# Self-attention and group norm on one core: all later row tiles in high/low parts, low parts on GpSimd, f and g in one step, y over x

## The chip, the cores and the metric

One core of a Trainium2 chip. Its engines are TensorE (matmuls, PE in the profile), VectorE (DVE), ScalarE (ACT), GpSimd (POOL) and SyncE (SP, which only issues transfers here). The metric is the device time of one execution in microseconds; lower is better.

## The reference

Eight images of 128 channels and 32 x 32 = 1024 positions, float32. First self-attention with a residual, then a group norm whose groups are found from the data.

```python
xf = x.reshape(B, Cc, N)                                  # B = 8, Cc = 128, N = 1024
x_f = jnp.einsum('oc,bcn->bon', Wf, xf) + bf[None, :, None]      # 16 rows
x_g = jnp.einsum('oc,bcn->bon', Wg, xf) + bg[None, :, None]      # 16 rows
x_h = jnp.einsum('oc,bcn->bon', Wh, xf) + bh[None, :, None]      # 128 rows
s = jnp.einsum('bci,bcj->bij', x_f, x_g)
beta = jax.nn.softmax(s, axis=-1)
x = x + gamma[0] * jnp.einsum('bci,bij->bcj', x_h, beta).reshape(B, Cc, H, W)
...
x_n = x_flat / jnp.maximum(nrm, 1e-12)
cos = jnp.einsum('bcn,bdn->cd', x_n, x_n) / B             # channels against channels
_, idx = jax.lax.top_k(-jnp.abs(cos).T, k)                # k = 4: the partners of a channel
mean, var over each channel and its 3 partners, per image
x_hat = (x - mean) * rsqrt(var + EPS);  out = gamma * x_hat + beta
```

## The kernel before, in words

The order on every engine is written out by hand, with semaphores between the engines. The images go one after the other; the stage of an image b has T = 8 steps t, one for each row tile of 128 rows of the 1024 x 1024 score matrix.

A row tile passes through these steps. TensorE scores it (`score`, two matmuls of 128x512 into one of two PSUM buffers `s_ps`). VectorE takes the negated row maximum (`row_max`). ScalarE takes exp with the row sum (`exp`, into `probs`). VectorE inverts the sum (`invert_sum`). The values of the tile are scaled by it, and TensorE multiplies them with the probabilities and adds to `o_ps` (`attend`). TensorE scores AHEAD = 3 tiles before the one it attends.

There are two forms of attend. A whole tile uses float32 operands: ScalarE scales the values (`scale_values`, into `vnorm`), and TensorE goes over each half in a slow float32 matmul. A split tile, here tiles 3 and 7 of each image (`SPLIT`), uses high and low parts in fp32r: ScalarE copies `probs` to `probs_high` (`high_part`), VectorE computes `probs_low = probs - probs_high`, `v_high = values * rinv` and `v_low = values * rinv - v_high` (`split_parts`), and TensorE does three fast products per half.

Beside the tiles a stage does the next image's projections into the PSUM tensor `w_ps`: f and g in one matmul per half (`project_fg`), which ScalarE copies to `fg32` (with the bias) and again, negated and masked, to `fg_neg`; g's rows are then added on VectorE (`parts`), f's rows on GpSimd (`parts_f`). The values of the next image follow (`project_values`, `add_value_bias`). For the previous image it does the residual (`residual`, from `x_all` to `y_all`), the squares and their norm (ScalarE and GpSimd, `nsq` and `rnorm`), and the product of y with itself: transposes, `yT` in a high part (ScalarE) and a low part (VectorE, `low_part`), `gram`, `scale_gram`, `turn_gram`, `add_gram`. After the last image the partners are found, and the shifted and scaled y is stored.

Of the kernel before, what the change touches and what calls it, by code (L numbers as in the profile page):

```python
# [37 lines left out]
P = 128  # L38
BANK = 512
AHEAD = 3  # L40
SCALED = 2
SPLIT = (3, 7)
# [9 lines left out]

def build(nc, x, wide, out):
# [4 lines left out]
    assert C == P and H == 2 and T == 8 and B % 2 == 0 and B >= 4  # L58
    assert all(SCALED <= t < T for t in SPLIT)

    with ExitStack() as ctx:
# [9 lines left out]
        x_all = sb("x_all", [P, B, N])  # L71
        y_all = sb("y_all", [P, B, N])
        wd = sb("wd", [P, WIDE])
        warm = sb("warm", [P, BANK], BF16)
        fg32 = sb("fg32", [P, N])
        fg_neg = sb("fg_neg", [P, N], F32R)
        f_parts = [sb(f"f_parts{i}", [P, N], F32R) for i in range(2)]
        g_parts = [sb(f"g_parts{i}", [P, N], F32R) for i in range(2)]
        values = [sb(f"values{i}", [P, T, P]) for i in range(2)]
        probs = [sb(f"probs{i}", [P, N]) for i in range(T)]  # L80
        vnorm = [sb(f"vnorm{i}", [P, P]) for i in range(T)]

        probs_high = [sb(f"probs_high{i}", [P, N], F32R) for i in range(len(SPLIT))]
        probs_low = [sb(f"probs_low{i}", [P, N], F32R) for i in range(len(SPLIT))]
        v_high = [sb(f"v_high{i}", [P, P], F32R) for i in range(len(SPLIT))]
        v_low = [sb(f"v_low{i}", [P, P], F32R) for i in range(len(SPLIT))]
# [43 lines left out]
        zeros_set = sem("zeros_set")  # L130

        fg_proj = sem("fg_proj")
        fg_copied = sem("fg_copied")
        neg_ready = sem("neg_ready")
        g_ready = sem("g_ready")
        f_head = sem("f_head")
        f_ready = sem("f_ready")
# [12 lines left out]
        probs_used = sem("probs_used")  # L150
# [31 lines left out]
        TH = T // H  # L182
        L = B - 1
# [8 lines left out]
        WHOLE = [t for t in range(T) if t not in SPLIT]  # L192

        def ahead(b, t, par):

            return (b, t, par) if t < T else (b + 1, t - T, 1 - par)

        def split_count(b, t):
            return len(SPLIT) * b + SPLIT.index(t) + 1

        def whole_count(b, t):
            return len(WHOLE) * b + WHOLE.index(t) + 1

        def run_stages(stage):

            for b in range(B):
                stage(b, b % 2, first=b == 0, previous=b > 0, turn=b > 1, project=b < L)

# [3 lines left out]
        def _(sp):  # L212
            for h in range(H):
                sp.dma_start(x_all[:, 0, halves[h]], x[0][:, halves[h]]).then_inc(head_in[h], 16)
            for b in range(1, B):
                if b == 2:

                    sp.wait_ge(const_in, 16)
                sp.dma_start(x_all[:, b, :], x[b]).then_inc(x_in[b], 16)
            sp.wait_ge(v_out, 1)  # L220
            sp.dma_start(out[0][:, halves[0]], y_all[:, 0, halves[0]]).then_inc(stored, 16)
            sp.wait_ge(a_head, 1)
            sp.dma_start(out[0][:, halves[1]], y_all[:, 0, halves[1]]).then_inc(stored, 16)
            for n, b in enumerate(VEC_IMAGES):
                sp.wait_ge(v_out, n + 2)
                sp.dma_start(out[b], y_all[:, b, :]).then_inc(stored, 16)
# [3 lines left out]
        def _(pool):  # L230
            nc.gpsimd.memset(mhalf[:, :], -0.5).then_inc(halves_set, 1)
            pool.wait_ge(halves_set, 1)

            def parts_f(b):
                for h in range(H):
                    pool.wait_ge(neg_ready, H * b + h + 1)
                    if b >= 2:

                        pool.wait_ge(scores, T * (b - 1))
                    nc.gpsimd.tensor_tensor(f_parts[b % 2][0:KP, halves[h]], fg32[0:KP, halves[h]],  # L240
                                            fg_neg[0:KP, halves[h]].bitcast(F32), ALU.add).then_inc(f_ready, 1)


            pool.wait_ge(neg_ready, H)
            pool.wait_ge(zeros_set, 4)
            nc.gpsimd.tensor_tensor(f_parts[0][0:KP, halves[1]], fg32[0:KP, halves[1]],
                                    fg_neg[0:KP, halves[1]].bitcast(F32), ALU.add).then_inc(f_ready, 1)
            for b in range(B):
                if b == 0:
                    parts_f(1)  # L250
# [509 lines left out]
```

## Time and profile before

| | |
|---|---|
| median of 3 runs | 213.6 us (213.32 to 213.78) |
| profiled execution, its own time | 213.6 us |
| its span | 211.8 us |
| one middle image | 22.2 us |
| TensorE busy | 88% of the span |
| VectorE busy | 82% |
| ScalarE busy | 68% |
| GpSimd busy | 16% |

The span is what the profiler recorded between the first and the last instruction of one execution; 1.8 us of the execution's own time lie outside it. Busy shares are averages over the head (loads and the first image), the middle and the tail, which have different limits.

### The profile page before, as it was taken

What the parts mean: (1) busy time and instruction counts of PE and PEld (TensorE: products, weight loads), DVE (VectorE), ACT (ScalarE), POOL (GpSimd) and SP (SyncE); (2) the same over time, 40 slices, a digit from 0 to 9 for tenths busy, and PEclk for the clock granted to TensorE, in tenths of its full rate; (3) what the DMA queues carried; (4) which work ended last, traced back from release to release, by engine and by line L of the source; (5) the groups of instructions that cost most, each with busy time, mean ns of one, the idle gap of its engine ahead of it and who ended that gap; (6) DMA issues with size and microseconds to landing.
All of it is one profiled execution on the core that took longest, in us unless ns stands there. A gap on an engine that the chain in (4) does not pass through costs nothing.

```text
span 211.8 us, 2308 instructions
## 1 busy us (share of the span) xinstructions
PE 187.0 (88%) x727; PEld 115.9 (55%) x727; DVE 174.3 (82%) x317; ACT 144.4 (68%) x256; POOL 34.4 (16%) x39
## 2 busy tenths in 40 slices
PE   7599979999999999999999999999999999983100
PEld 2454546465765676566756675667566756371000
DVE  6678989979898889989898989888988898766650
ACT  2548976799379955995599658985799378740320
POOL 0200210034003400160007000520034001001400
PEclk9969999999999999999999999999999999996555
DMA  5880000000000000000000000000000000000198
GB/s 209 315 330 0 0 3 0 3 0 0 0 3 0 0 0 0 0 3 2 0 0 2 0 0 3 0 0 0 0 3 2 0 0 0 0 3 2 57 400 335
DMA packets 2892, 8.87 MB, mean 42 GB/s; under 512 B 320, under 2 KB 448, under 8 KB 2880
## 3 DMA queue, kind: packets, MB, share of 16 engines
q1 hardware_dynamic: 2304, 7.34, 9.0%
q10 hardware_dynamic: 576, 1.38, 1.7%
q8 instruction: 6, 0.10, 0.2%
q14 instruction: 6, 0.05, 0.1%
HBM read 4.52 MB, written 4.19 MB: 41 GB/s over the span
## 4 chain that ended last, share of the span: by engine, by line
PE 73%; DVE 11%; ACT 6%; issue 5%; POOL 1%; DVEq 0%; ACTq 0%; POOLq 0%
PE o_ps L602 40%; PE s_ps L583 12%; PE w_ps L572 7%; PE w_ps L577 6%; PE w_ps L617 3%; PE w_ps L611 2%; DVE nmax L376 2%; ACT probs L292 2%; PE o_ps L569 2%; DVE y_all L562 1%; DVE probs_low L390 1%; DVE g_parts L399 1%; DVE y_all L414 1%; ACT probs_high L298 1%; ACT fg_neg L285 1%
## 5 line engine op out<-in xcount | busy, mean ns | idle before, releaser
L292 ACT ACTIVATE probs<-s_ps,nmax 128x1024 f32<-128x1024 f32 x64 | 71.0, 1109 | 40.4 <-DVE nmax L376 40.2
L602 PE MATMUL o_ps<-probs,vnorm 128*128 128x512 f32 x192 | 89.9, 592 | 0.5 <-DVE y_all L414 0.5
L376 DVE TENSOR_REDUCE nmax<-s_ps 128x1 f32<-128x1024 f32 x64 | 78.0, 1220 | 12.8 <-PE s_ps L583 12.3
L583 PE MATMUL s_ps<-g_parts,f_parts 128*128 128x512 f32 x128 | 52.0, 489 | 3.8 <-DVE g_parts L399 2.2
L602 PEld LDWEIGHTS o_ps<-probs,vnorm 128*128 128x128 f32 x192 | 35.7, 189 | 28.0 <-issue 22.8
L240 POOL TENSOR_TENSOR f_parts<-fg,fg_neg 64x512 fp32r<-64x512 f32 x14 | 24.0, 1715 | 122.2 <-ACT fg_neg L285 122.2
L583 PEld LDWEIGHTS s_ps<-g_parts,f_parts 128*128 128x128 f32 x128 | 21.4, 191 | 20.1 <-issue 15.1
L390 DVE TENSOR_TENSOR probs_low<-probs,probs_high 128x1024 fp32r<-128x1024 f32 x16 | 19.5, 1220 | 1.4 <-ACT probs_high L298 1.3
L309 ACT ACTIVATE vnorm<-values,rinv 128x128 f32<-128x128 f32 x48 | 18.8, 392 | 0.0
L577 PEld LDWEIGHTS w_ps<-wd,x_all 128*128 128x128 f32 x112 | 14.7, 192 | 6.7 <-issue 6.7
L399 DVE TENSOR_TENSOR g_parts<-fg,fg_neg 64x512 fp32r<-64x512 f32 x16 | 14.0, 872 | 4.9 <-ACT fg_neg L285 4.1
L572 PE MATMUL w_ps<-x_all,wd 128*128 128x512 f32 x32 | 17.6, 647 | 0.0
L298 ACT ACTIVATE probs_high<-probs 128x1024 fp32r<-128x1024 f32 x16 | 16.8, 1048 | 0.0
L577 PE MATMUL w_ps<-wd,x_all 128*128 128x128 f32 x112 | 14.8, 275 | 0.0
L602 PE MATMUL o_ps<-probs_high,v_high 128*128 128x512 f32 x32 | 12.7, 398 | 0.1
L602 PE MATMUL o_ps<-probs_high,v_low 128*128 128x512 f32 x32 | 12.7, 396 | 0.0
L282 ACT ACTIVATE fg<-w_ps,wd 128x512 f32<-128x512 f32 x16 | 10.8, 676 | 2.5 <-PE w_ps L572 2.5
L602 PE MATMUL o_ps<-probs_low,v_high 128*128 128x512 f32 x32 | 12.5, 390 | 0.0
L292 ACT ACTIVATION_READ_ACCUMULATOR probs<-s_ps,nmax 128x1 f32 x64 | 12.4, 193 | 0.0
L285 ACT ACTIVATE fg_neg<-fg,wd 128x512 fp32r<-128x512 f32 x16 | 11.6, 723 | 0.5
L572 PEld LDWEIGHTS w_ps<-x_all,wd 128*128 128x128 f32 x32 | 6.6, 208 | 7.9 <-issue 6.8
L380 DVE RECIPROCAL rinv<-rsum 128x1 f32<-128x1 f32 x64 | 10.0, 156 | 1.1 <-ACT probs L292 0.4
(90 smaller groups left out, 169.2 us busy)
## 6 DMA issues: line engine op xcount, KB each, us to landing
x_all<-x_dram SPq DMA_DIRECT2D x7, 512.0 KB, 6.1
out_dram<-y_all SPq DMA_DIRECT2D x5, 512.0 KB, 5.8
out_dram<-y_all ACTq DMA_DIRECT2D x2, 512.0 KB, 4.1
x_all<-x_dram SPq DMA_DIRECT2D x2, 256.0 KB, 3.7
out_dram<-y_all SPq DMA_DIRECT2D x2, 256.0 KB, 2.2
wd<-wide_dram ACTq DMA_DIRECT2D x1, 256.0 KB, 4.3
wd<-wide_dram ACTq DMA_DIRECT2D x1, 66.5 KB, 3.4
```

Of the source, the lines that this page charges most:

```text
L240: nc.gpsimd.tensor_tensor(f_parts[b % 2][0:KP, halves[h]], fg32[0:KP, halves[h]], fg_neg[0:KP, halves[h]].bitcast(F32), ALU.add).then_inc( ...
L285: nc.scalar.activation(fg_neg[:, halves[h]], fg32[:, halves[h]], ACT.Copy, scale=wd[:, NMASK:NMASK + 1]).then_inc(neg_ready, 1)
L292: nc.scalar.activation(probs[t][:, :], s_ps[t % 2][:, :], ACT.Exp, bias=nmax[:, t:t + 1], accum_out=rsum[:, t:t + 1]).then_inc(exp_done, 1)
L298: nc.scalar.activation(probs_high[SPLIT.index(t)][:, :], probs[t][:, :], ACT.Copy).then_inc(high_ready, 1)
L309: nc.scalar.activation(vnorm[t][:, :], values[par][:, t, :], ACT.Copy, scale=rinv[:, t:t + 1]).then_inc(vn_ready, 1)
L376: nc.vector.reduce_max(nmax[:, t:t + 1], s_ps[t % 2][:, :], AX_X, negate=True).then_inc(max_ready, 1)
L390: nc.vector.tensor_tensor(probs_low[n][:, :], probs[t][:, :], probs_high[n][:, :].bitcast(F32), ALU.subtract).then_inc(low_ready, 1)
L399: nc.vector.tensor_tensor(to[0:KP, columns], fg32[rows, columns], fg_neg[rows, columns].bitcast(F32), ALU.add).then_inc(done, 1)
L572: return nc.tensor.matmul(w_ps[:, halves[h]], wd[:, WFG:WFG + P], x_all[:, b, halves[h]], start=True, stop=True)
L577: last = nc.tensor.matmul(to[:, t * P:(t + 1) * P], source[:, t * P:(t + 1) * P], wd[:, WHT:WHT + P], start=True, stop=True)
L583: last = nc.tensor.matmul(s_ps[t % 2][:, h], f_parts[par][:, t * P:(t + 1) * P], g_parts[par][:, h], start=True, stop=True)
L602: last = nc.tensor.matmul(o_ps[:, halves[h]], weights[:, :], rows[:, halves[h]], start=(t == 0 and n == 0), stop=(t == T - 1 and n == len( ...
```

## The change

From the second image on all eight row tiles are split; in the first image tiles 0, 1, 2 and 4 stay whole (`WHOLE_FIRST`). The low part of the probabilities is computed on GpSimd instead of VectorE. TensorE scores four tiles ahead; in the first image a table says how many tiles are scored at each step (`SCORED_FIRST`). `fg32` is gone: ScalarE makes the negated part from PSUM directly, and VectorE makes f's and g's rows in one step of 128 partitions, also from PSUM; the g rows are then moved to partitions 0 to 63 by a transfer on SyncE's queue. y is written over x (`xy`). There are six buffers for probabilities and five for their parts. The previous image's transposes are done at once at step 2, its gram product at step 6 of the same stage, and the residual at step 0 of the next.

```diff
-AHEAD = 3
+AHEAD = 4
-SPLIT = (3, 7)
+PROBS = 6
+PARTS = 5
+WHOLE_FIRST = (0, 1, 2, 4)
+WHOLE_LATER = ()
+SCORED_FIRST = (3, 4, 6, 7, 9, 10, 11, 12)
+    def is_split(n):
+        return n % T not in (WHOLE_FIRST if n < T else WHOLE_LATER)
...
         @block.sync
+            for b in range(1, B):
+                for h in range(H):
+                    sp.wait_ge(parts_ready, H * b + h + 1)
+                    sp.dma_start(g_rows[b % 2][f_rows, halves[h]].bitcast(F32),
+                                 fg_parts[b % 2][g_part_rows, halves[h]].bitcast(F32)).then_inc(g_moved[h], 16)
...
         @block.gpsimd
-            def parts_f(b):
-                    nc.gpsimd.tensor_tensor(f_parts[b % 2][0:KP, halves[h]], fg32[0:KP, halves[h]],
-                                            fg_neg[0:KP, halves[h]].bitcast(F32), ALU.add).then_inc(f_ready, 1)
+            def low_part(n):
+                i = split_at[n]
+                pool.wait_ge(high_ready, i + 1)
+                nc.gpsimd.tensor_tensor(probs_low[i % PARTS][:, :], probs[n % PROBS][:, :],
+                                        probs_high[i % PARTS][:, :].bitcast(F32),
+                                        ALU.subtract).then_inc(low_ready, 1)
+            for n in SPLIT_TILES:
+                low_part(n)
+                b, t = divmod(n, T)
+                if b > 0 and t == 5:
+                    invert_norm(b - 1)
...
         @block.scalar
-            def copy_fg(b, h):
-                nc.scalar.activation(fg32[:, halves[h]], w_ps[:, halves[h]], ACT.Identity,
-                                     bias=wd[:, BFG:BFG + 1]).then_inc(fg_copied, 1)
-                nc.scalar.activation(fg_neg[:, halves[h]], fg32[:, halves[h]], ACT.Copy,
-                                     scale=wd[:, NMASK:NMASK + 1]).then_inc(neg_ready, 1)
+            def negate_high(b, h):
+                nc.scalar.activation(fg_neg[:, halves[h]], w_ps[:, halves[h]], ACT.Identity,
+                                     bias=low_bias[:, 0:1], scale=wd[:, NMASK:NMASK + 1]).then_inc(neg_ready, 1)
...
         @block.vector
-            def split_parts(b, t, par):
-                nc.vector.tensor_scalar(v_high[n][:, :], values[par][:, t, :], rinv[:, t:t + 1], None,
-                                        ALU.mult).then_inc(vh_ready, 1)
-                nc.vector.tensor_tensor(probs_low[n][:, :], probs[t][:, :], probs_high[n][:, :].bitcast(F32),
-                                        ALU.subtract).then_inc(low_ready, 1)
-                nc.vector.scalar_tensor_tensor(v_low[n][:, :], values[par][:, t, :], rinv[:, t:t + 1],
+            def split_values(n):
+                dve.wait_ge(rinv_ready, n + 1)
+                dve.wait_ge(v_ready, H * b + t // TH + 1)
+                nc.vector.tensor_scalar(v_high[t][:, :], values[b % 2][:, t, :], rinv[:, t:t + 1], None,
+                                        ALU.mult).then_inc(vh_ready, 1)
+                dve.wait_ge(vh_ready, split_at[n] + 1)
+                nc.vector.scalar_tensor_tensor(v_low[t][:, :], values[b % 2][:, t, :], rinv[:, t:t + 1],
+                                               v_high[t][:, :].bitcast(F32), ALU.mult,
+                                               ALU.subtract).then_inc(vl_ready, 1)
+            def parts(to, rows, h, done):
+                nc.vector.scalar_tensor_tensor(to, w_ps[rows, halves[h]], wd[rows, BFG:BFG + 1],
+                                               fg_neg[rows, halves[h]].bitcast(F32), ALU.add,
+                                               ALU.add).then_inc(done, 1)
...
         @block.tensor
+            def attend(n):
+                if is_split(n):
+                    pe.wait_ge(vl_ready, i + 1)
+                    pe.wait_ge(low_ready, i + 1)
```

On VectorE, this is a stretch of a middle image before: the end of the stage's step 0 up to step 2 (`v_high`, `probs_low` and `v_low` belong to a split tile, `nmax` is the row maximum, `rinv` the inverse sum).

```order
L376 TENSOR_REDUCE nmax<-s_ps 128x1
L380 RECIPROCAL rinv<-rsum 128x1
L387 TENSOR_SCALAR v_high<-values,rinv 128x128
L390 TENSOR_TENSOR probs_low<-probs,probs_high 128x1024
L393 SCALAR_TENSOR_TENSOR v_low<-values,rinv,v_high 128x128
L436 SCALAR_TENSOR_TENSOR half_cos<-w_ps,rnorm,half_cos 128x128
L376 TENSOR_REDUCE nmax<-s_ps 128x1
L380 RECIPROCAL rinv<-rsum 128x1
L399 TENSOR_TENSOR g_parts<-fg,fg_neg 64x512
```

And this is the stretch from step 1 to step 3 of a middle image now.

```order
L402 SCALAR_TENSOR_TENSOR fg_parts<-w_ps,wd,fg_neg 128x512
L382 TENSOR_REDUCE nmax<-s_ps 128x1
L387 RECIPROCAL rinv<-rsum 128x1
L393 TENSOR_SCALAR v_high<-values,rinv 128x128
L396 SCALAR_TENSOR_TENSOR v_low<-values,rinv,v_high 128x128
L382 TENSOR_REDUCE nmax<-s_ps 128x1
L387 RECIPROCAL rinv<-rsum 128x1
L393 TENSOR_SCALAR v_high<-values,rinv 128x128
L396 SCALAR_TENSOR_TENSOR v_low<-values,rinv,v_high 128x128
L423 TENSOR_TENSOR yT<-w_ps,yT 128x4x128 x2
```

`v_high` and `v_low` now stand behind every row maximum, and `probs_low` is gone from the engine.

On GpSimd, the difference between the two programs from the start of the first image's work to the second image's norm: f's rows (`f_parts`) went, the low parts came.

```order
-L240 TENSOR_TENSOR f_parts<-fg,fg_neg 64x512 x4
-L256 TENSOR_SCALAR nsq<-stats 128x1
-L263 TENSOR_TENSOR rnorm<-nsq,mhalf 128x1
-L240 TENSOR_TENSOR f_parts<-fg,fg_neg 64x512 x2
```

```order
+L249 MEMSET g_rows 64x1024 x2
+L256 ISA
+L256 TENSOR_TENSOR probs_low<-probs,probs_high 128x1024 x10
+L263 TENSOR_SCALAR nsq<-stats 128x1
+L270 TENSOR_TENSOR rnorm<-nsq,mhalf 128x1
+L256 TENSOR_TENSOR probs_low<-probs,probs_high 128x1024 x8
```

Eight subtractions of 128x1024 stand between one image's norm and the next, where two additions of 64x512 stood.

## Rows read from the trace of the kernel before

**Rows 1.** The page: busy us, share of the span and instructions of each engine.

```profile
PE 187.0 (88%) x727; PEld 115.9 (55%) x727; DVE 174.3 (82%) x317; ACT 144.4 (68%) x256; POOL 34.4 (16%) x39
```

**Rows 2.** Table by stage: us, busy us (x instructions) of PE, PEld, DVE, ACT, POOL; clock, DMA.

```profile
81.60:103.80 22.20, 22.20 (x91) 14.14 (x90) 19.62 (x36) 17.36 (x32) 4.33 (x4) 1.00 0.00 1
170.00:187.00 17.00, 16.91 (x60) 9.65 (x59) 13.97 (x28) 11.46 (x22) 1.00 (x2) 1.00 0.00 0
```

**Rows 3.** The chain that ended last: start us, us, what.

```profile
87.21 1.72 PE o_ps L602 x4
90.24 1.39 PE o_ps L602 x6
...
169.39 1.43 DVE y_all L414 x4
```

**Rows 4.** Timeline of VectorE in a middle image: start us, us, operation.

```profile
83.13 0.33 DVE L427 TENSOR_SCALAR gram_high<-w_ps,rnorm 128x128 f32<-128x128 f32 x1
83.50 0.35 DVE L430 SCALAR_TENSOR_TENSOR gram_rows<-w_ps,rnorm,gram_high 128x128 f32<-128x128 f32 x1
83.77 0.68 DVE L407 TENSOR_TENSOR values<-w_ps,wd 128x512 f32<-128x512 f32 x1
84.36 1.22 DVE L376 TENSOR_REDUCE nmax<-s_ps 128x1 f32<-128x1024 f32 x1
85.50 0.15 DVE L380 RECIPROCAL rinv<-rsum 128x1 f32<-128x1 f32 x1
85.69 0.29 DVE L387 TENSOR_SCALAR v_high<-values,rinv 128x128 fp32r<-128x128 f32 x1
...
87.02 0.35 DVE L393 SCALAR_TENSOR_TENSOR v_low<-values,rinv,v_high 128x128 fp32r<-128x128 f32 x1
87.28 0.35 DVE L436 SCALAR_TENSOR_TENSOR half_cos<-w_ps,rnorm,half_cos 128x128 f32<-128x128 f32 x1
```

**Rows 5.** Timeline of ScalarE in the same image.

```profile
84.58 1.04 ACT L298 ACTIVATE probs_high<-probs 128x1024 fp32r<-128x1024 f32 x1
85.52 1.05 ACT L322 ACTIVATE squares<-y_all 128x1024 f32<-128x1024 f32 x1
...
86.56 1.10 ACT L292 ACTIVATE probs<-s_ps,nmax 128x1024 f32<-128x1024 f32 x1
87.56 0.20 ACT L292 ACTIVATION_READ_ACCUMULATOR probs<-s_ps,nmax 128x1 f32 x1
```

**Rows 6.** Timeline where GpSimd and VectorE meet, and nsq undisturbed at 115.85.

```profile
8.60 1.25 POOL L246 TENSOR_TENSOR f_parts<-fg,fg_neg 64x512 fp32r<-64x512 f32 x1 [7.77 <-ACT fg_neg L285]
8.67 1.73 DVE L399 TENSOR_TENSOR g_parts<-fg,fg_neg 64x512 fp32r<-64x512 f32 x1
...
44.98 0.69 DVE L399 TENSOR_TENSOR g_parts<-fg,fg_neg 64x512 fp32r<-64x512 f32 x1 [0.77 <-ACT fg_neg L285]
45.02 1.80 POOL L240 TENSOR_TENSOR f_parts<-fg,fg_neg 64x512 fp32r<-64x512 f32 x1 [17.50 <-ACT fg_neg L285]
...
115.85 0.21 POOL L256 TENSOR_SCALAR nsq<-stats 128x1 f32<-128x1 f32 x1
...
174.77 1.22 DVE L390 TENSOR_TENSOR probs_low<-probs,probs_high 128x1024 fp32r<-128x1024 f32 x1
...
175.63 0.43 POOL L256 TENSOR_SCALAR nsq<-stats 128x1 f32<-128x1 f32 x1 [14.47 <-ACT squares L322]
```

**Rows 7.** DMA issues: KB each, median us from issue to landing.

```profile
x_all<-x_dram SPq DMA_DIRECT2D x2, 256.0 KB, 3.7
```

**Rows 8.** The chain again, in the head and in the tail.

```profile
5.69 0.70 ACT fg L282
...
187.02 0.96 PE w_ps L617 x8
```

**Rows 9.** A stage of the head in the table by stage; TensorE's wait before it.

```profile
10.00:14.00 4.00, 3.50 (x7) 1.91 (x8) 3.95 (x5) 1.11 (x2) 0.00 (x0) 0.67 1.01 409
...
10.50 0.47 PE L583 MATMUL s_ps<-g_parts,f_parts 128*128 128x512 f32 x1 [2.25 <-DVE g_parts L399]
```

More of the change, by code:

```diff
@@ L57, in build, with scored_before, newly_scored @@
     KP = 4 * 16
-    assert C == P and H == 2 and T == 8 and B % 2 == 0 and B >= 4
-    assert all(SCALED <= t < T for t in SPLIT)
+    TH = T // H
+    L = B - 1
+    TILES = T * B
+    assert C == P and H == 2 and T == 8 and B >= 3
+    def is_split(n):
+        return n % T not in (WHOLE_FIRST if n < T else WHOLE_LATER)
+    SPLIT_TILES = [n for n in range(TILES) if is_split(n)]
+    WHOLE_TILES = [n for n in range(TILES) if not is_split(n)]
+    split_at = {n: i for i, n in enumerate(SPLIT_TILES)}
+    whole_at = {n: i for i, n in enumerate(WHOLE_TILES)}
+    def scored_before(b, t):
+        return min(SCORED_FIRST[t] if b == 0 else T * b + t + AHEAD + 1, TILES)
+    def newly_scored(b, t):
+        before = SCORED_FIRST[0] if b == 0 and t == 0 else scored_before(*divmod(T * b + t - 1, T))
+        return range(before, scored_before(b, t))
     with ExitStack() as ctx:
@@ new lines, in _ @@
+            act.wait_ge(wfg_in, 16)
+            act.wait_ge(bias_ready, 1)
+            for h in range(H):
+                negate_high(0, h)
+            exp(0)
+            exp(1)
+            scale_values(0)
+            exp(2)
+            scale_values(1)
+            for b in range(B):
+                for t in range(T):
+                    if t < 2 and b < L:
+                        negate_high(b + 1, t)
+                    for n in newly_scored(b, t):
+                        exp(n)
+                        if is_split(n):
+                            high_part(n)
+                    n = T * b + t + SCALED
+                    if n < TILES and not is_split(n):
+                        scale_values(n)
+                    if t == 0 and b > 0:
@@ L397, in parts, with row_max @@
[L397 to L404 removed]
+            def row_max(n):
+                dve.wait_ge(scores, n + 1)
+                nc.vector.reduce_max(nmax[:, n % T:n % T + 1], s_ps[n % 2][:, :], AX_X,
+                                     negate=True).then_inc(max_ready, 1)
@@ L592, in attend @@
                 for h in range(H):
-                    if after is not None:
-                        pe.wait_ge(y_ready, H * (after - 1) + h + 1)
-                    if t in SPLIT:
-                        n = SPLIT.index(t)
-                        products = [(v_high[n], probs_high[n]), (v_low[n], probs_high[n]), (v_high[n], probs_low[n])]
-                    else:
-                        products = [(vnorm[t], probs[t])]
-                    for n, (weights, rows) in enumerate(products):
+                    if t == 0 and b > 0:
+                        pe.wait_ge(y_ready, H * (b - 1) + h + 1)
@@ L606, in attend @@
+                    if h == 0 and n == TILES - 1:
                         last.then_inc(first_half, 1)
-                last.then_inc(probs_used, 1)
+                last.then_inc(attended, 1)
             def transposes(source, to, tiles, first=0):
```

427 lines of the change are left out of this document (185 added, 242 removed).

## The prediction

> **What bounds the kernel now.** I read the busy shares first. TensorE is busy 88% of the span and VectorE 82%, ScalarE 68%, GpSimd 16% [rows 1]. A share over the whole span says little, so the table by stage comes next: in one middle image (22.20 us, from one row maximum to the same one an image later) TensorE is busy 22.20 us, VectorE 19.62, ScalarE 17.36, GpSimd 4.33, at full granted clock [rows 2]. In the images between 37.2 and 170.4 us, six of them at 22.2 us, nothing but TensorE ends last. The chain of waits gives its prices: a whole tile attended (four passes) 1.72 us, a tile in high/low parts (six faster ones) 1.39 us [rows 3]. VectorE has only 2.6 us per image to spare, and that is the number to watch. The profiled execution took 213.6 us, the same as the median, so the sum is made against 213.6.
>
> **TensorE.** Six more tiles per image become split, each saving 1.72 - 1.39 = 0.33 us: 22.2 - 2.0 = 20.2 us per image. It stops being the bound if anything else needs more.
>
> **VectorE.** I price by the distance from one start to the next, since neighbouring instructions overlap a little [rows 4]. A row maximum takes 84.36 to 85.50 = 1.14; reciprocal to v_high 0.19; v_low to the next instruction 0.26. v_low now waits for v_high directly; the same kind of pair, gram_high and gram_rows, starts 0.37 apart with 0.33 of duration, so 0.28 of v_high plus 0.04 = 0.32. Per tile: 1.14 + 0.19 + 0.32 + 0.26 = 1.91, or 15.3 per image. Call the rest O: residual 1.43 [rows 3]; two steps for f and g together, two for values, two low parts of yT, each a half read from PSUM, at the 0.59 of the values (83.77 to 84.36); gram 0.37 + 0.27 + 0.27 [rows 4]. O is 1.43 + 6 x 0.59 + 0.91 = 5.9 per image, 0.74 per tile on average. Sum 21.2 us against 19.6 before: two 1.2 us subtractions go to GpSimd, six pairs of v_high and v_low come in, and f and g together cost what g alone did. If nothing else happened VectorE would replace TensorE as the bound at 21.2.
>
> **ScalarE.** An exp with its accumulator read ends 1.20 after its start (86.56 to 87.76), and the high part, which waits for it, follows 0.03 later [rows 5]; the high part is 1.05 long, 0.95 to the next start. 8 x (1.23 + 0.95) = 17.4, plus squares at 1.04 (85.52 to 86.56), yT, which has the same shape, at the same, and two negated steps of 128x512 at the 0.70 of the fg copy [rows 8]: 20.9 us. The separate copies to fg and the six vnorm scalings disappear. Close to the others, but not above VectorE.
>
> **GpSimd.** Its new operation is a subtraction of 128x1024 with two SBUF inputs. The nearest row is its 64x512 addition: 1.25 us when nothing is in its way [rows 6]. Twice that is 2.50; if a start as long as its 128x1 instruction (0.21) is paid once only, 2.29. I take 2.35. Eight of them, with 0.8 for the norm, are 19.6 us per image, also under 22.2. By work alone every engine would fit into 21.2.
>
> **What the two engines do to each other.** This is the term that decides. At 8.60 us GpSimd starts its addition; VectorE starts its own addition of two SBUF tensors 0.07 us later and takes 1.73 us instead of 0.69. It ends at 10.40, 0.55 after GpSimd's end at 9.85: it stood still until GpSimd had finished. At 44.98 VectorE is first by 0.04 us, keeps its 0.69, and GpSimd takes 1.80 instead of 1.25. At 175.63 GpSimd's tiny nsq starts inside VectorE's subtraction of probs_low and takes 0.43 instead of 0.21 [rows 6]. So whoever is second waits for the whole instruction of the first. Row maxima, residuals, values and the new f/g step read PSUM and at most one SBUF tensor, and so do the low parts of yT: before, g_parts and probs_low were the long exposed ones, now they are gone. But v_low (values and v_high, both SBUF) stands in every tile, and GpSimd now holds the path for 2.35 us in every tile instead of 3.6 us per image.
> The Trainium skill, "SBUF — State Buffer", section "Who interferes with whom", states this as an exclusive lock on a port pair shared by the two engines; on that rule the trace agrees. The page adds that a tensor_scalar in a two-port mode takes the lock too. That would put v_high among the blocked ones as well, 29.0 us per image in the sum below instead of 27.7. From the rows alone: v_high takes 0.29 where v_low takes 0.35 over the same 128 columns [rows 4], as if it read them faster than one at a time; whether it waits for GpSimd no row shows, so both values bound the sum.
>
> **The walk through a tile.** Put a row maximum at 0. It ends at 1.23 (its duration, 1.22, and 0.01 for the semaphore), exp follows 0.03 later (near 1.26), the high part at 2.49, and GpSimd's low part starts 1.05 + 0.03 later, at 3.57, to run until 5.92. VectorE goes on meanwhile: v_low of the next step is asked for at 1.91 + O + w + 1.65 = 3.56 + O + w, with w the wait already suffered in this step, and v_high 0.32 before. With O of 0.74 and no wait that is 4.30, inside GpSimd's run. The next wait is then 5.92 - 3.56 - (O + w) = 2.36 - (O + w). Averaged over many tiles, O + w = (2.36 + 0.74) / 2 = 1.55: a tile takes 1.91 + 1.55 = 3.46 us and an image 27.7. If v_high is blocked too, the 2.36 becomes 2.68, O + w 1.71, a tile 3.62 and an image 29.0. I take 28.2, 6.0 us more than now. The four tiles of lead don't help, since the wait is on VectorE's own queue: behind v_low stand the row maxima, exp behind them, and the scores behind exp.
> Before, the two engines met only twice per image, at the f and g additions.
>
> **The other edits.** The g rows are moved to partitions 0 to 63 by two transfers per image on SyncE's queue, 128 KB each; a 256 KB load takes 3.7 us to land [rows 7], and from the second f/g step to the first score of the next image lie two tiles, over 5.3 us. I cost it at nothing; if VectorE ran at 2.65 a tile some 1 us of cover would be left. Loads are over by then, and the stores come later. The head loses a ScalarE copy (0.70 [rows 8]) and VectorE's blocked addition (1.04 of its 1.73 [rows 6]), and the second g step stands one ScalarE copy less deep: -2.0. In the tail the gram product of 0.96 us no longer stands between the last tile and the transposes [rows 8], of which 0.6 was on the path (the residual hides the rest). y over x only frees SBUF for six probability buffers. In image 0 and the last image TensorE has gaps already (16.91 busy in 17.0, and VectorE 13.97 there [rows 2]); about five split tiles' waits of 0.9 each fall on a slack of about half: +5 together.
> Sum: 213.6 + 6 x 6.0 - 2.0 - 0.6 + 5 = 252.0 us.
>
> **Rivals.**
> Back to back: GpSimd falls behind, always has the next subtraction ready, and VectorE's two instructions slip between. A tile is then 2.35 + 0.25 + 0.30 = 2.90, an image 23.2 + 0.8 = 24.0: 213.6 + 6 x 1.8 - 2.6 + 2 = 224. For it: four tiles of lead let GpSimd lag. Against: v_low needs v_high's result, so between them a waiting GpSimd instruction goes first.
> Caught twice: exactly that. Where O + w is under about 0.6 (six of the eight O are 0 to 0.64 by the code's order), v_high is freed at 5.92, GpSimd's next subtraction is ready by then, and v_low waits 2.35 more. A pair of tiles then has 4.4 us of waits; were it all pairs, 4.85 us a tile and 39 us an image. Half of them: 33.5, and 213.6 + 6 x 11.3 - 2.6 + 5 = 284.
> No waits (the other side): v_low with a pointer scalar and 128 columns passes GpSimd as PSUM readers do. VectorE's 21.2 is the bound: 213.6 + 6 x (21.3 - 22.2) - 2.6 = 206. It decides below a mean wait of (22.2 - 21.2) / 8 = 0.12 us per tile. For it: no row shows v_low or v_high beside a running subtraction of GpSimd; against: the three pairs above.
> Slow TensorE: the granted clock was 0.67 on average between 10 and 14 us, so at its lower level (1.2 instead of 2.4 GHz) for two thirds of that time, behind a wait of TensorE of 2.25 us [rows 9]. TensorE would have 8 us of gaps per image; at half clock all the time its 20.2 would be 40.4 us. A third of the time gives 26.9, still hidden under 28.2, so only a larger share costs: 270 or more.
> There, the Trainium skill, "TensorE: Matmul & The Clock Gate", section "HAM oscillation — how this bites in real kernels", warns that long gaps lower the clock; no gap in the walk is over 2.4 us, and the 22.2 us images here show none.
>
> **Numbers.** Single waits, 238 to 266 us: 0.45. Back to back, 219 to 238: 0.17. Caught twice or a slow TensorE, above 266: 0.22. No waits: 0.14. The last 0.02 is a draw. The likeliest gives 252; the range 219 to 286 holds the first two and most of the third. The measurement can tell 0.2%, and only the no-wait case is faster: 0.14 faster, 0.02 same, 0.84 slower.
>
> **What would show it.** VectorE's v_low (and perhaps v_high) with a mean over 0.8 us instead of 0.35, always ending just behind a GpSimd subtraction; those subtractions at 2.3 to 2.5 us alone and some 0.25 longer when second; split tiles still 1.39 on TensorE; TensorE busy near 20 us in an image of 28; a chain of waits that runs over VectorE, ScalarE and GpSimd. Wrong would be: v_low at 0.35 throughout, or a subtraction on GpSimd well over 2.5 us, which would make GpSimd itself the bound, or TensorE waiting for the moved g rows.

## The result and the profile after

The changed kernel takes 277.35 us (four runs, 277.01 to 278.03) against 213.6: the ratio is 1.299 [1.2961, 1.3019], 64 us slower. The forecast was 252.0 us in a range of 219 to 286: right way, inside the range, and 25 us short. Its profiled execution took 277.24 us with a span of 275.4. Ratios here and below use only runs within 1.5% of the fastest of their kernel, which leaves out two of e7's four, the profiled one among them.

The page of the changed kernel, its busy shares and the chain that ended last by engine and line, answers to [rows 1]:

```profile
PE 200.1 (73%) x815; PEld 144.2 (52%) x815; DVE 241.5 (88%) x387; ACT 172.1 (63%) x240; POOL 154.1 (56%) x86
...
DVE 62%; issue 16%; PE 16%; ACT 2%; POOL 1%; DVEq 0%; ACTq 0%; POOLq 0%
DVE v_high L393 22%; DVE nmax L382 21%; PE o_ps L607 5%; PE s_ps L588 4%; PE w_ps L569 3%; DVE yT L423 3%; DVE values L413 3%; DVE v_low L396 3%; DVE rinv L387 2%; DVE fg_parts L402 2%; PE o_ps L566 1%; ACT probs L304 1%; DVE xy L418 1%; DVE xy L559 1%; DVE gram_rows L432 1%
```

VectorE took TensorE's place on the chain, and 22% of the chain, about 60 us, is one instruction of 128x128 elements, v_high. A caught v_low hides in the 16% of "issue": where one stands on the chain, at 129.53, it is a piece of 0.04 us with 2.40 us of "issue" behind it. The costliest groups of the same page show what it does there (count, then busy us, mean ns of one, idle time before):

```profile
L256 POOL TENSOR_TENSOR probs_low<-probs,probs_high 128x1024 fp32r<-128x1024 f32 x60 | 143.2, 2393 | 94.7 <-ACT probs_high L313 93.9
...
L393 DVE TENSOR_SCALAR v_high<-values,rinv 128x128 fp32r<-128x128 f32 x60 | 63.8, 1064 | 2.1
...
L396 DVE SCALAR_TENSOR_TENSOR v_low<-values,rinv,v_high 128x128 fp32r<-128x128 f32 x60 | 40.2, 669 | 2.1
```

In a free stretch v_high takes 0.29 us and v_low 0.35 [rows 4]; here they average 1.06 and 0.67. With the 0.287 and 0.351 that they take in e2, where nothing stops them, that is (1.064 - 0.287) x 60 = 46.6 and (0.669 - 0.351) x 60 = 19.1 us, 65.7 us of standing still that is booked as VectorE's busy time. Its 88% is not 88% of work. The same view of v_high and v_low one by one (minimum/median/maximum) says that it is the caught ones that are long; 36 of the 60 v_high and 9 of the 60 v_low are over 0.4 us, and each of these 45 ends 0.08 to 0.15 us behind the end of a GpSimd subtraction:

```profile
L393 DVE TENSOR_SCALAR v_high<-values,rinv x60: 285/1143/2262, 21.4 to 247.3; 128x128 fp32r<-128x128 f32 x60
L396 DVE SCALAR_TENSOR_TENSOR v_low<-values,rinv,v_high x60: 350/352/2555, 21.7 to 247.6; 128x128 fp32r<-128x128 f32 x60
```

The timelines of GpSimd and of VectorE over the same 8 us of a middle image (start us, us) put the two side by side:

```profile
119.43 2.37 POOL L256 TENSOR_TENSOR probs_low<-probs,probs_high 128x1024 fp32r<-128x1024 f32 x1
...
122.57 2.38 POOL L256 TENSOR_TENSOR probs_low<-probs,probs_high 128x1024 fp32r<-128x1024 f32 x1 [0.77 <-ACT probs_high L313]
127.01 4.89 POOL L256 TENSOR_TENSOR probs_low<-probs,probs_high 128x1024 fp32r<-128x1024 f32 x2 [2.06 <-ACT probs_high L313]
```

```profile
120.27 1.62 DVE L393 TENSOR_SCALAR v_high<-values,rinv 128x128 fp32r<-128x128 f32 x1
121.92 0.35 DVE L396 SCALAR_TENSOR_TENSOR v_low<-values,rinv,v_high 128x128 fp32r<-128x128 f32 x1
...
124.71 0.32 DVE L393 TENSOR_SCALAR v_high<-values,rinv 128x128 fp32r<-128x128 f32 x1
...
127.25 2.24 DVE L393 TENSOR_SCALAR v_high<-values,rinv 128x128 fp32r<-128x128 f32 x1
...
129.53 2.52 DVE L396 SCALAR_TENSOR_TENSOR v_low<-values,rinv,v_high 128x128 fp32r<-128x128 f32 x1
```

GpSimd's subtraction ends at 119.43 + 2.37 = 121.80, and the v_high that was asked for at 120.27 ends at 121.89. The one at 124.71 ends at 125.03, behind GpSimd's end at 124.95. At 127.25 v_high is caught behind the first of two subtractions that follow each other directly, and v_low, 0.04 us behind it, is caught by the second: 2.24 + 2.52 us for 0.64 us of work. (The row of 4.89 us is two subtractions, 127.01 to 129.41 and 129.56 to 131.90.) The row maximum at 123.39 reads PSUM and keeps its 1.21 us beside a running subtraction.

The table by stage of one middle image, from its residual to the next (us; busy of PE, PEld, DVE, ACT, POOL with instructions; granted clock), answers to [rows 2], and two rows of its chain to [rows 3]:

```profile
137.04:168.14 31.10, 24.66 (x101) 18.47 (x101) 29.42 (x46) 21.16 (x31) 19.90 (x11) 0.86 0.04 9
```

```profile
140.29 2.52 PE o_ps L607 x6
...
148.13 1.63 DVE v_high L393
```

The 31.1 us are made of 8.6 us of caught v_high and v_low (13.69 us busy for 8 x 0.64), 1.1 us in which the row maxima wait for scores of a TensorE at a low granted clock (below), and 21.4 us that are left for VectorE's own work with the small gaps in it. Against before: the first image's residual starts at 44.87 instead of 36.44 (+8.4); the next six images take 30.7 us on average instead of 22.2 (184.4 against 133.0, +51.5); what is left after that takes 46.1 instead of 42.4 (+3.7). That is the 63.6 us between the spans.

### The profile page after: what moved, and what is told of

It reads as the page before. It is cut to its first block, busy times and chain, and to the rows that moved or that the text cites. A ratio compares the mean times of both kernels' runs of the same rounds, so it can differ in the third digit from the quotient of the medians.

```text
span 275.4 us, 2732 instructions
## 1 busy us (share of the span) xinstructions
PE 200.1 (73%) x815; PEld 144.2 (52%) x815; DVE 241.5 (88%) x387; ACT 172.1 (63%) x240; POOL 154.1 (56%) x86
## 4 chain that ended last, share of the span: by engine, by line
DVE 62%; issue 16%; PE 16%; ACT 2%; POOL 1%; DVEq 0%; ACTq 0%; POOLq 0%
DVE v_high L393 22%; DVE nmax L382 21%; PE o_ps L607 5%; PE s_ps L588 4%; PE w_ps L569 3%; DVE yT L423 3%; DVE values L413 3%; DVE v_low L396 3%; DVE rinv L387 2%; DVE fg_parts L402 2%; PE o_ps L566 1%; ACT probs L304 1%; DVE xy L418 1%; DVE xy L559 1%; DVE gram_rows L432 1%
## 5 line engine op out<-in xcount | busy, mean ns | idle before, releaser
L256 POOL TENSOR_TENSOR probs_low<-probs,probs_high 128x1024 fp32r<-128x1024 f32 x60 | 143.2, 2393 | 94.7 <-ACT probs_high L313 93.9
L607 PE MATMUL o_ps<-probs_high,v_high 128*128 128x512 f32 x120 | 59.1, 493 | 16.1 <-DVE v_low L396 13.3
L393 DVE TENSOR_SCALAR v_high<-values,rinv 128x128 fp32r<-128x128 f32 x60 | 63.8, 1064 | 2.1
L313 ACT ACTIVATE probs_high<-probs 128x1024 fp32r<-128x1024 f32 x60 | 63.5, 1059 | 1.9
L588 PE MATMUL s_ps<-g_rows,fg_parts 128*128 128x512 f32 x128 | 48.4, 465 | 6.9 <-ACT probs L304 6.2
L607 PE MATMUL o_ps<-probs_high,v_low 128*128 128x512 f32 x120 | 51.1, 426 | 0.0
L607 PE MATMUL o_ps<-probs_low,v_high 128*128 128x512 f32 x120 | 50.9, 424 | 0.0
L396 DVE SCALAR_TENSOR_TENSOR v_low<-values,rinv,v_high 128x128 fp32r<-128x128 f32 x60 | 40.2, 669 | 2.1
L607 PEld LDWEIGHTS o_ps<-probs_high,v_high 128*128 128x128 f32 x120 | 25.1, 209 | 30.6 <-DVE v_low L396 21.7
L607 PEld LDWEIGHTS o_ps<-probs_high,v_low 128*128 128x128 f32 x120 | 25.1, 209 | 8.6 <-issue 4.0
L569 PE MATMUL w_ps<-xy,wd 128*128 128x512 f32 x32 | 22.3, 794 | 1.2 <-DVE half_cos L438 1.2
```

The source lines that it names most:

```text
L256: nc.gpsimd.tensor_tensor(probs_low[i % PARTS][:, :], probs[n % PROBS][:, :], probs_high[i % PARTS][:, :].bitcast(F32), ALU.subtract).then ...
L313: nc.scalar.activation(probs_high[i % PARTS][:, :], probs[n % PROBS][:, :], ACT.Copy).then_inc(high_ready, 1)
L393: nc.vector.tensor_scalar(v_high[t][:, :], values[b % 2][:, t, :], rinv[:, t:t + 1], None, ALU.mult).then_inc(vh_ready, 1)
L396: nc.vector.scalar_tensor_tensor(v_low[t][:, :], values[b % 2][:, t, :], rinv[:, t:t + 1], v_high[t][:, :].bitcast(F32), ALU.mult, ALU.sub ...
L569: nc.tensor.matmul(w_ps[:, halves[h]], wd[:, WFG:WFG + P], xy[:, b, halves[h]], start=True, stop=True).then_inc(fg_proj, 1)
L588: last = nc.tensor.matmul(s_ps[n % 2][:, h], fg_parts[b % 2][:, t * P:(t + 1) * P], g_rows[b % 2][:, h], start=True, stop=True)
```

## The experiments

Two theories stood at the start: the loss comes from VectorE and GpSimd shutting each other out of SBUF; or it comes from GpSimd delivering the low parts late, so that TensorE and everything behind it waits, with v_high and v_low long only as a symptom. Times are medians; each ratio is against runs of the kernel before on the same chip (213.6 to 213.7 us).

**e1: all low parts back on VectorE.**

```diff
         @block.gpsimd
-            for n in SPLIT_TILES:
-                low_part(n)
...
         @block.vector
             def split_values(n):
...
                 nc.vector.tensor_scalar(v_high[t][:, :], values[b % 2][:, t, :], rinv[:, t:t + 1], None,
                                         ALU.mult).then_inc(vh_ready, 1)
+                i = split_at[n]
+                dve.wait_ge(high_ready, i + 1)
+                nc.vector.tensor_tensor(probs_low[i % PARTS][:, :], probs[n % PROBS][:, :],
+                                        probs_high[i % PARTS][:, :].bitcast(F32),
+                                        ALU.subtract).then_inc(low_ready, 1)
                 dve.wait_ge(vh_ready, split_at[n] + 1)
                 nc.vector.scalar_tensor_tensor(v_low[t][:, :], values[b % 2][:, t, :], rinv[:, t:t + 1],
...
```

> The low parts of the probabilities go back to VectorE (between v_high and v_low), all else as changed; GpSimd then does only the norms. Theory (v_high and v_low wait for GpSimd's running subtraction): v_high back to 0.29 us and v_low to 0.35, no wait left, but VectorE's own work rises from 21.2 to 21.2 + 8 x 1.13 = 30.2 us per image, so an image takes about 30.4 us and the whole 270 to 277 us. Rival (the low parts are late on GpSimd, 2.39 us each, and TensorE waits for them): the subtraction takes half as long on VectorE, v_high keeps its long duration, and the time falls clearly, below 260.

Measured: 273.12 us, ratio 1.2787 [1.2724, 1.285]. Its v_high and v_low, one by one, and its table by stage over one image:

```profile
L383 DVE TENSOR_SCALAR v_high<-values,rinv x60: 285/287/291, 21.3 to 242.1; 128x128 fp32r<-128x128 f32 x60
L391 DVE SCALAR_TENSOR_TENSOR v_low<-values,rinv,v_high x60: 340/345/348, 23.4 to 243.5; 128x128 fp32r<-128x128 f32 x60
```

```profile
134.36:164.73 30.37, 23.24 (x103) 17.77 (x102) 29.19 (x56) 21.18 (x29) 0.79 (x2) 0.89 0.04 9
```

No instruction is caught any more, yet the kernel is only 4 us faster than the changed one. Eight subtractions at 1.14 us from start to start on top of the forecast's 21.2 are 30.3 us, and an image takes 30.4. The agreement is partly luck: 0.9 us of the image are row maxima that wait for scores (0.17 and 0.70), so VectorE's own part is 29.5; with a subtraction between them v_high and v_low cost 0.1 us less per tile, since the next instruction starts 0.20 us behind v_high instead of 0.32. Moving 143 us of subtraction off to GpSimd bought less than nothing: the two engines together take 4 us longer than VectorE alone.

**e2: the subtractions left out.** The low parts are zeros set once; no engine subtracts. TensorE does all its products.

```diff
-            for n in SPLIT_TILES:
-                low_part(n)
+            for i in range(PARTS):
+                nc.gpsimd.memset(probs_low[i][:, :].bitcast(F32), 0.0).then_inc(low_ready, 1)
...
         @block.tensor
-                    pe.wait_ge(low_ready, i + 1)
+                    pe.wait_ge(high_ready, i + 1)
+                    pe.wait_ge(low_ready, PARTS)
```

> The low parts of the probabilities are left out: their buffers are set to zero once and TensorE still does the product with them. Theory: without GpSimd's subtractions v_high and v_low take 0.29 and 0.35 us, an image falls from 31.1 to 21.2 to 21.8 us, VectorE the bound, and the whole to 211 to 217 us. Rival (VectorE's own work was priced too low, or TensorE's lower clock is what costs): the image stays above 26 us, the whole above 245.

Measured: 218.45 us, 1.0228 [1.0193, 1.0263], 1.5 us above the theory's range and far below the rival's. One image by stage:

```profile
85.50:108.13 22.63, 20.87 (x102) 16.23 (x101) 20.92 (x46) 20.94 (x30) 0.79 (x2) 1.00 0.06 13
```

The whole effect of the subtractions on GpSimd is thus 277.35 - 218.45 = 58.9 us, beside 65.7 us of caught time. It also shows that the other edits are not a gain even so: 22.6 us an image, where the forecast's walk has 21.2 for VectorE's work. Two waits of VectorE for ScalarE, 0.5 us each, at fg_neg and yT, are 1.0 of the 1.4 us between.

**e3: v_high in a form with an accumulator.** The same product, with a sum nobody reads.

```diff
-                nc.vector.tensor_scalar(v_high[t][:, :], values[b % 2][:, t, :], rinv[:, t:t + 1], None,
-                                        ALU.mult).then_inc(vh_ready, 1)
+                nc.vector.tensor_scalar(v_high[t][:, :], values[b % 2][:, t, :], rinv[:, t:t + 1], 0.0,
+                                        ALU.mult, ALU.add, accum_out=vsum[:, t:t + 1]).then_inc(vh_ready, 1)
```

> v_high is made by a tensor_scalar that also writes an accumulator, with GpSimd's subtractions in place. Theory with the rule that the plain form waits because it reads with both ports: this form, about 0.35 us long, no longer waits, v_low alone does, with a mean of 0.35 + about 0.8 us; an image 28.3 us, the whole near 260. Rival (any VectorE instruction that reads SBUF waits for GpSimd): v_high still has a mean near 1.06 us and the time stays near 277.

Measured: 273.16 us, 1.2789 [1.276, 1.2818]. One by one:

```profile
L394 DVE TENSOR_SCALAR_CACHE_REDUCE v_high<-values,rinv x60: 345/346/349, 21.5 to 242.9; 128x128 fp32r<-128x128 f32 x60
...
L397 DVE SCALAR_TENSOR_TENSOR v_low<-values,rinv,v_high x60: 350/1096/2524, 21.9 to 243.3; 128x128 fp32r<-128x128 f32 x60
```

This form takes 0.346 us instead of 0.287 and is never caught, not once in 60, though 38 of the 60 start inside a running subtraction. But v_low behind it now is: its mean goes from 669 to 1175 ns. Caught time falls from 65.7 to (1.175 - 0.351) x 60 = 49.4 us, 60 x (0.059 + 0.083) = 8.5 us of work comes in (the form and its accumulator read), and of the 7.8 us that should be left, 4.2 are seen. The theory held for v_high, and the time was missed by 13 us: a wait passed over by v_high is taken up by v_low.

**e4: v_high and v_low left out,** with GpSimd's subtractions kept as they are; TensorE multiplies zeros set once.

```diff
+            for i in range(T):
+                nc.vector.memset(v_high[i][:, :].bitcast(F32), 0.0).then_inc(vl_ready, 1)
+                nc.vector.memset(v_low[i][:, :].bitcast(F32), 0.0).then_inc(vl_ready, 1)
...
-                        if is_split(n):
-                            split_values(n)
...
         @block.tensor
-                    pe.wait_ge(vl_ready, i + 1)
+                    pe.wait_ge(vl_ready, 2 * T)
+                    pe.wait_ge(rinv_ready, n + 1)
```

> v_high and v_low are left out (set to zero once, so the attended sum is left out for split tiles), GpSimd's subtractions stay. It is the other half of the pair: if GpSimd alone is late, the time stays high; if only the meeting of the two engines costs, it falls as far as it did without the low parts. Theory (meeting): subtractions still 2.39 us, an image between 20.9 and 22.7 us, the whole 208 to 219 us. Rival (GpSimd's 2.39 us per tile is too long for TensorE's lead of four tiles): above 240.

Measured: 212.92 us, 0.9968 [0.9951, 0.9984]. The group of the subtractions, and one image by stage:

```profile
L256 POOL TENSOR_TENSOR probs_low<-probs,probs_high 128x1024 fp32r<-128x1024 f32 x60 | 142.2, 2398 | 34.6 <-ACT probs_high L313 34.4
```

```profile
82.11:103.86 21.75, 20.66 (x101) 16.31 (x101) 16.07 (x31) 20.88 (x30) 19.71 (x11) 1.00 0.06 13
```

GpSimd does the same 60 subtractions of 2.4 us, and an image takes 21.8 us. VectorE has 5 us of work less in it as well, so this time is not a bound for the full kernel, but it shows that GpSimd and everything behind it can keep such a pace; the second theory falls. Either side of the pair can be taken out, e2 or e4, and the loss goes.

**e7: GpSimd's subtraction also waits for the previous split tile's v_low.** No work is changed, only when GpSimd starts.

```diff
                 pool.wait_ge(high_ready, i + 1)
+                if i > 0:
+                    pool.wait_ge(vl_ready, i)
```

> All as changed, but GpSimd's subtraction for a tile also waits until VectorE's v_low of the split tile before it in order is done, so that it starts in VectorE's longest free stretch. Theory (only the phase of the meetings costs): v_low back near 0.35 us, v_high with a mean near 0.85 us or less, no tile with two waits, an image 25.8 to 27.5 us and the whole 243 to 256 us. Rival (each subtraction costs VectorE a fixed wait, or the extra wait on GpSimd makes it the bound): 270 us or more.

Measured: 246.8 us (245.52 and 248.07; all four runs lie between 245.52 and 250.76), 1.1549 [1.1478, 1.162]; the profiled execution took 250.76. Groups:

```profile
L258 POOL TENSOR_TENSOR probs_low<-probs,probs_high 128x1024 fp32r<-128x1024 f32 x60 | 143.0, 2384 | 70.7 <-DVE v_low L398 46.5 <-ACT probs_high L315 24.2
L395 DVE TENSOR_SCALAR v_high<-values,rinv 128x128 fp32r<-128x128 f32 x60 | 44.6, 744 | 2.1
L398 DVE SCALAR_TENSOR_TENSOR v_low<-values,rinv,v_high 128x128 fp32r<-128x128 f32 x60 | 23.1, 385 | 2.1
```

A wait added to GpSimd makes the kernel about 30 us faster. 43 of the 60 v_high still wait, but more briefly (0.74 us on average instead of 1.06), one single v_low is caught, and no pair waits twice: the subtraction now often starts right behind a pair of v_high and v_low and has run for some time when the next pair comes. Caught time falls from 65.7 to (0.457 + 0.034) x 60 = 29.5 us. Only the timing of the two engines was changed, so that much of the loss is in their meeting.

**e6: two split tiles as before, low parts on VectorE,** so that only the other edits remain (`WHOLE_LATER = (0, 1, 2, 4, 5, 6)`, `WHOLE_FIRST` the same, and e1's edit).

> The other edits alone: tiles 3 and 7 of each image split and their low parts on VectorE as before, with four tiles of lead, f and g in one step, y over x and the new places of transposes, gram and residual. All theories: TensorE is the bound again at 22.2 us per image, the head is 1.5 to 2 us and the tail 0.5 us shorter: 210.5 to 212.5 us.

Measured: 224.28 us, 1.0503 [1.0478, 1.0528]: missed by 12 us. One matmul of the gram product, once an image:

```profile
110.63 0.30 PE L623 MATMUL w_ps<-wd,gram_rows 128*128 128x128 f32 x1 [0.75 <-DVE gram_rows L427]
```

The edits that the forecast took as free or as a gain cost 10.7 us. An image takes 23.1 us instead of 22.2, of which TensorE waits 0.75 for gram_rows, which stand behind step 7's row maximum. The first image ends at 41.60 instead of 36.44; in it scores wait 5.3 us for exp (two waits), where they waited 1.5 before.

**e10: e6 with the gram scaled ahead of step 7's row maximum.**

```diff
+                    if t == 7 and b > 0:
+                        scale_gram(b - 1, w_ps)
                     for n in newly_scored(b, t):
                         row_max(n)
...
-                    if t == 7 and b > 0:
-                        scale_gram(b - 1, w_ps)
```

> As the run with two split tiles on VectorE, but the scaling of the gram product stands before the row maximum of step 7 instead of behind it. Theory (the boundary wait of 0.75 us and the work behind it is TensorE waiting for gram_rows, which stands behind a row maximum): the wait on L623 goes, an image falls from 23.1 to 22.2 us, the whole from 224.3 to 218.5 to 220. Rival (the stall is the w_ps buffer itself): no change.

Measured: 218.29 us, 1.0213 [1.0196, 1.023]. An image takes 22.1 us, TensorE is busy in all of it: 6.0 us of e6's 10.7 went with this one move. The first image still ends at 40.95, and that is the 4.6 us which are left.

**e11: e2 with the same move,** again without the subtractions.

> Low parts of the probabilities left out (buffers zero), and the scaling of the gram product ahead of the row maximum of step 7. It asks what VectorE's 22.6 us per image without GpSimd are made of, against the 21.2 that its instructions sum to. If TensorE's wait for gram_rows is behind it, an image falls to 21.5 to 22 us and the whole from 218.5 to 212 to 215. If the 1.4 us are VectorE's waits for ScalarE (fg_neg, yT and a probability), nothing changes: 217.5 to 219.

Measured: 218.53 us, 1.0229 [1.0207, 1.0251], the same as e2, with 22.6 us an image. With eight split tiles the gram is not what VectorE's image hangs on. The two waits of 0.5 us for ScalarE are still there; no run takes them away, so that they are what holds the image at 22.6 is argued.

**b1: the kernel before with three split tiles,** `SPLIT = (3, 5, 7)`.

> The kernel before with one more split tile, 3, 5 and 7, all low parts on VectorE. TensorE saves 0.33 us per image (21.9), VectorE rises from 19.6 busy to about 21.3, still below. Theory (TensorE's sum): 213.6 - 8 x 0.33 = 211 us, or down to no change if VectorE's waits eat it. Rival (VectorE's queue is already the hidden bound): 214 to 217.

Measured: 220.9 us, 1.0319 [1.0289, 1.035], where 211 was expected and the rival had 214 to 217. Three rows of its timeline:

```profile
97.06 1.40 POOL L240 TENSOR_TENSOR f_parts<-fg,fg_neg 64x512 fp32r<-64x512 f32 x1 [1.87 <-ACT fg_neg L285]
97.25 1.36 DVE L393 SCALAR_TENSOR_TENSOR v_low<-values,rinv,v_high 128x128 fp32r<-128x128 f32 x1
...
99.43 0.47 PE L583 MATMUL s_ps<-g_parts,f_parts 128*128 128x512 f32 x1 [0.56 <-issue]
```

One more split tile, which should have saved TensorE 0.33 us, makes an image 22.7 us instead of 22.2 and the first image 3.2 us longer. VectorE gets another 1.7 us (high and low part and subtraction) and 1.0 us of a v_low that GpSimd's f addition catches, once in each of six images: 2.7 us against its 2.6 to spare. The kernel before seems to stand near the limit of its VectorE queue; the row of TensorE's own wait (0.56 us, "issue") doesn't name what ended it, so this is argued.

**b2: the kernel before, with GpSimd's first f addition held back behind VectorE's g additions.**

```diff
             pool.wait_ge(zeros_set, 4)
+            pool.wait_ge(g_ready, H)
             nc.gpsimd.tensor_tensor(f_parts[0][0:KP, halves[1]], fg32[0:KP, halves[1]],
```

> The kernel before, with one wait added: in the head GpSimd's addition for f (64x512, 1.25 us at 8.60) starts only when both g additions of VectorE are done. Theory (the 1.04 us by which VectorE's addition stood still at 8.67 lie on the chain to the first score): that addition takes 0.69 us, the first score starts near 9.4 instead of 10.5, and the time is 212.4 to 213.0 us. Rival (a later wait in the first image takes it back): 213.4 to 213.8.

Measured: 212.5 us (six runs, 211.88 to 212.97), 0.9946 [0.9929, 0.9964]. Its timeline at the place of [rows 6]:

```profile
9.03 0.69 DVE L400 TENSOR_TENSOR g_parts<-fg,fg_neg 64x512 fp32r<-64x512 f32 x1
...
9.82 1.16 PE L584 MATMUL s_ps<-g_parts,f_parts 128*128 128x512 f32 x4 [1.23 <-DVE g_parts L400]
9.89 1.27 POOL L247 TENSOR_TENSOR f_parts<-fg,fg_neg 64x512 fp32r<-64x512 f32 x1 [9.06 <-DVE g_parts L400]
```

The blocked g addition takes 0.69 us instead of 1.73, the first score starts 0.7 us earlier (this execution makes its first g addition 0.35 us later than before, at 7.59), and the first residual 1.35 us earlier (35.09). With 1.1 us, 0.5%, this one wait beats both kernels.

**e9: the changed kernel with what was learned:** four split tiles (`WHOLE_LATER = (1, 3, 5, 7)`), e7's wait, the gram scaled first (and GpSimd's norm one tile sooner, behind tile 4).

> The changed kernel repaired as far as the runs suggest: tiles 1, 3, 5 and 7 whole from the second image on, GpSimd's subtraction behind the v_low before it, the scaling of the gram product first. TensorE 20.2 + 4 x 0.33 = 21.5 us per image, VectorE 4 x 1.91 + 4 x 1.21 + 5.9 = 18.4 plus waits of about 0.5 for each of four tiles, 20.4: TensorE the bound. The first image stays 3 us longer than before, so 211 to 215 us. Rival (any subtraction on GpSimd costs more than it saves here): above 218.

Measured: 217.26 us, 1.0159 [1.0142, 1.0177], between the two theories. v_high has a mean of 352 ns and v_low of 414, so all but 4 us of the caught time is gone; an image takes 22.3 us, and the first image ends at 40.36, 3.9 us later than before. The subtractions can live beside VectorE, but then they no longer pay.

## Why the prediction was right in kind and short in size

**What bounds after.** The forecast had VectorE in TensorE's place by its own work alone, at 21.2 us; in the image of the table it has 21.4 us. GpSimd's subtraction was put at 2.35 and takes 2.39. For ScalarE and TensorE it had 20.9 and 20.2; in e2 they are busy 20.9 each. These terms stood, TensorE's 0.7 us short. As the bound without any meeting 21.2 was too low: e2 has 22.6 an image, 1.0 of it VectorE's waits for ScalarE, which the sum of one engine's work doesn't hold. The table of the changed kernel's image shows none of them.

**The meeting.** Right: the second of the two waits until the whole instruction of the first has ended (121.80 and 121.89), the row maximum, a reader of PSUM, passes, and both v_high and v_low are stopped. Of the forecast's two cases it is the one with v_high, which the rows of before left open: alone 0.287 us, 1.58 on average over the 36 caught, and in e3 a form that takes 0.346 was never caught. The Trainium skill, "SBUF — State Buffer", section "Who interferes with whom", says this of the two-port modes, which a tensor_scalar can enter and its form with an accumulator cannot; the traces agree with both halves. Most of the wait fell on v_high (46.6 of 65.7 us), so that v_low's mean is 0.67 us, under the 0.8 that the forecast gave as its sign, and v_high's above it.

**The step that was mis-sized: "I take 28.2".** An image takes 30.7 on average, 6 x 2.5 = 15 us of the missing 25. With v_high blocked, which it is, the forecast's own walk gives 29.0, so 0.8 us of the 2.5 is the weight that it gave to the case of v_low alone. In the image shown, waits of v_high and v_low come to 8.6 us, where 28.2 - 21.2 leaves 7.0. The forecast held "caught twice" as a rival and gave it none of the sum; it happens in this kernel, once in each of the six middle images (127.25 and 158.36 are two of them) and once in the first, and each time costs 2.2 us more than one catch. Without it the image's waits are 6.4 us, close to the walk. The likeliest case should have been a mixture: neither the single waits nor the rival describes the run. Another 1.1 us are TensorE's.

**TensorE's clock.** The forecast's walk had no gap over 2.4 us and the full clock. The waits of the changed kernel by releaser (us in total, times, longest):

```profile
PEld o_ps L607 <- DVE v_low L396: 21.7, 13, 3.6
...
PE w_ps L628 <- DVE gram_rows L432: 16.9, 6, 3.5
```

The longest waits for gram_rows, 3.5 us, are over the forecast's 2.4, and the granted clock is 0.86 over the image, which is the lower of the two levels (1.2 instead of 2.4 GHz) for 28% of it; a split tile takes 2.52 us there instead of 1.39. The level falls behind shorter waits too. These are two stretches ahead of this image by stage, and two matmuls with TensorE's waits before them:

```profile
129.00:132.00 3.00, 1.07 (x8) 0.63 (x6) 2.96 (x3) 0.48 (x1) 2.76 (x2) 1.00 0.00 0
132.00:134.50 2.50, 2.39 (x6) 1.61 (x6) 2.43 (x7) 0.68 (x1) 0.00 (x0) 0.58 0.00 0
...
132.11 0.57 PE L607 MATMUL o_ps<-probs_high,v_high 128*128 128x512 f32 x1 [2.04 <-DVE v_low L396]
...
137.27 0.45 PE L628 MATMUL w_ps<-wd,gram_rows 128*128 128x128 f32 x1 [2.46 <-DVE gram_rows L432]
```

TensorE waits 2.04 us for the v_low that is caught twice, the level falls, and the wait for gram_rows (2.46 us) comes after that, at the lower level. So the forecast's premise that a walk without a gap over 2.4 us keeps the full clock fell, and here it is the double catch that goes ahead of the fall. The forecast's rival of a slow TensorE allowed for a third of the time and had it hidden; it is hidden but for the row maxima's 1.1 us (0.17 and 0.91). In e1, with the same level for some of its image (0.89), row maxima wait 0.9. No run holds the clock up with the rest unchanged, so what it costs over the whole kernel is read, not tested.

**First and last image, head and tail.** The forecast summed these to -2.0 - 0.6 + 5 = +2.4; they came to 8.4 + 3.7 = +12.1, the other 10 us of the miss. By e2, which has the same edits without the subtractions, the parts are +3.0 for the first image where -2.0 stood, -0.6 for what is left behind the middle images (41.8 us against 42.4), as forecast, and +9.7 that come with the catches at both ends (5.4 and 4.3) where +5 stood. The +5 rested on a slack of TensorE that its row doesn't show: 16.91 us busy in 17.0 is no gap [rows 2]. The head's gain was there but small: the first score starts at 9.72 instead of 10.50, not 2.0 earlier, since the second g step now stands behind f's step on VectorE (from 8.08) and starts at 8.86, 0.2 us later than before. Only the block of 1.0 us is gained. Of the first image's 8.4 us, e2 leaves 3.0 without any subtraction; the other 5.4 come with 7.1 us of catches in this image, among them v_low three times at 2.3 to 2.4 us. The 3.0 go with scores that wait for exp: 4.6 us in e2 and 1.5 before. With four tiles scored ahead, exp's queue is asked for more in image 0; that this order is the cause was argued from those waits, and no run changed `AHEAD` by itself.

**"The other edits" at nothing or less.** This fell. With two split tiles and no subtraction on GpSimd they cost 10.7 us (e6), 6.0 of it the gram scaled behind a row maximum (e10). The forecast never priced where scale_gram stands on VectorE. With eight split tiles and no subtraction this place costs nothing (e11 equals e2), so of the 25 us only the first image's part is shown to belong here. The moved g rows, though, cost nothing that shows: 2.2 us to land on the page, and TensorE waits for none of them.

**The rivals.** No waits (206 us) is out: 36 of 60 v_high are caught. Back to back (224) is out as well: GpSimd does not lag, it idles 93.9 us waiting for probs_high. A late GpSimd is out by e4.

## What to carry to other kernels

Before an elementwise operation is moved from VectorE to GpSimd, list which of VectorE's other instructions are of the kinds that waited here (two inputs in SBUF, or a plain tensor_scalar from SBUF), and count how often one of them falls due inside GpSimd's instruction: short ones, asked for once a tile, each cost the rest of a long one. If the two must meet, start the long one directly behind the short ones; one added wait was worth about 30 us here, and 1.1 us in the kernel before. A busy time that grows while the work is the same was waiting time here, and the sum of an engine's work is only a lower bound where the order of its queue is fixed.

## What was not expected of the hardware

A pair of dependent VectorE instructions can lose twice: v_low needs v_high's result, and a GpSimd subtraction that is ready gets its turn between them (127.25: 2.24 and 2.52 us). The forecast named this as a rival; that it comes once in every middle image was not expected. The recorded starts don't show who won: v_low starts at 129.53 and the subtraction at 129.56, and yet it is v_low that waits, as its 2.52 us beside the subtraction's 2.35 show. And the same product with an accumulator takes 0.346 us instead of 0.287, plus 0.083 for its read, and is never stopped by GpSimd; the faster form is the one that waits, and yet the slower one gained only 4 us, since v_low took over the wait.
